# Mixture routes: two doubling ladders replaced by scans, tile sums laid out expert by expert

## The reference, cut to what matters

```python
raw_weights = softmax(flat_x @ gate_w + gate_b)          # mixture 0
top_w, top_idx = top_k(raw_weights, 2)
...
_, topk_idx = top_k(probs, 2)                            # mixture 1
for i in range(N_EXPERTS):
    mask = (topk_idx == i).any(-1)
    sel = sort(where(mask, tok, T))[:capacity]
    ...
    out = out.at[sel].set(yi, mode='drop')
```

## Time and profile before

| what | value |
|---|---|
| median of 3 runs | 2750.04 us (2747.57 to 2751.27) |
| the profiled execution | 2749.84 us |
| its span in the profile | 2748.1 us |
| busy share of PE, DVE, ACT, POOL | 90%, 73%, 57%, 47% |
| mean granted clock of TensorE | 0.946 of full speed |

### The profile page before, as it was taken

The page is one execution under the profiler, slowest core; times in us unless marked ns, Lnnn a source line. Parts: engine busy times, 40 slices in busy tenths (PEclk is TensorE's granted clock), DMA queues, the critical chain, the costliest instruction groups (busy, mean ns, idle before and its releaser), DMA issues. The chain is left out here.

```text
span 2748.1 us, 54258 instructions
## 1 busy us (share of the span) xinstructions
PE 2467.7 (90%) x20834; PEld 1914.0 (70%) x20834; DVE 2001.7 (73%) x2977; ACT 1572.5 (57%) x2642; POOL 1294.0 (47%) x738
## 2 busy tenths in 40 slices
PE   4879939999978999857999999999999999956998
PEld 3658839999977878744666666666666666546998
DVE  5775567888868866537777777777777777277886
ACT  4554426777755543323666666666666666634775
POOL 0000002222224301334888888888888888802443
PEclk9999969999999999986999999999999999957999
DMA  9985325666656754335000000040000000055775
GB/s 394 367 337 182 121 78 202 239 228 231 232 172 217 235 192 128 112 99 127 17 11 15 17 9 17 9 91 11 15 17 9 17 11 13 2 149 190 239 236 139
DMA packets 112303, 352.23 MB, mean 128 GB/s; under 512 B 21424, under 2 KB 53424, under 8 KB 94704
## 3 DMA queue, kind: packets, MB, share of 16 engines
q1 hardware_dynamic: 88432, 289.79, 30.8%
q0 software_dynamic: 22096, 55.07, 7.7%
q10 hardware_dynamic: 1584, 4.75, 0.4%
HBM read 308.40 MB, written 41.16 MB: 127 GB/s over the span
## 5 line engine op out<-in xcount | busy, mean ns | idle before, releaser
L1233 POOL TENSOR_TENSOR at_pool_sum<-at_pool_sum,at_probs 128x1024 f32<-128x1024 f32 x364 | 866.1, 2379 | 97.1 <-ACT at_probs L1359 55.5
L1388 DVE TENSOR_REDUCE at_part_max<-ps_x 128x2 f32<-128x1024 f32 x624 | 734.5, 1221 | 227.7 <-PE ps_x L1289 227.7
L1359 ACT ACTIVATE at_probs<-ps_s 128x512 f32<-128x512 f32 x1352 | 698.2, 604 | 323.8 <-PE ps_s L1248 295.6
L1248 PE MATMUL ps_s<-at_qst,at_kst 97*128 97x256 f32 x2704 | 517.9, 311 | 5.4 <-ACT at_probs L1359 4.3
L1248 PEld LDWEIGHTS ps_s<-at_qst,at_kst 97*128 97x128 f32 x2704 | 369.3, 190 | 218.1 <-ACT at_probs L1359 125.7
L1265 PE MATMUL ps_oz<-at_probs,k_xhat 128*32 128x256 f32 (+1 forms) x5408 | 391.4, 386 | 0.0
L477 PE MATMUL ps_acc<-adj_hi,y_hi 128*128 128x512 f32 (+1 forms) x728 | 289.8, 398 | 93.0 <-DVE adj_lo L543 62.2
L543 DVE TENSOR_TENSOR adj_lo<-adj_raw,adj_hi 128x1024 fp32r<-128x1024 f32 (+1 forms) x182 | 217.7, 1198 | 165.1 <-ACT adj_hi L319 162.8
L479 PE MATMUL ps_acc<-adj_hi,y_lo 128*128 128x512 f32 (+1 forms) x728 | 278.1, 382 | 0.0
L478 PE MATMUL ps_acc<-adj_lo,y_hi 128*128 128x512 f32 (+1 forms) x728 | 278.0, 382 | 0.0
L937 ACT ACTIVATE ex_hid<-ps_ex_h,ex_b 128x256 f32<-128x256 f32 x424 | 193.4, 475 | 124.3 <-PE ps_ex_h L878 113.2
(11 more groups left out here) (223 smaller groups left out, 3998.7 us busy)
## 6 DMA issues: line engine op xcount, KB each, us to landing
ex_w<-w SPq DMA_DIRECT2D x106, 1024.0 KB, 7.7
adj_raw<-adjT SPq DMA_DIRECT2D x156, 512.0 KB, 4.4
k_xhat<-adj SPq DMA_DIRECT2D x26, 1664.0 KB, 7.7
at_qst<-qk_parts SPq DMA_DIRECT2D x78, 128.0 KB, 2.7
results<-ex_res POOLq DMA_DIRECT2D x33, 256.0 KB, 3.3
ex_b<-b SPq DMA_DIRECT2D x53, 128.0 KB, 2.3
adj_raw<-adjT_tail SPq DMA_DIRECT2D x26, 256.0 KB, 2.7
qk_parts<-qk_hi POOLq DMA_DIRECT2D x26, 256.0 KB, 2.8
```

The source lines that it names most:

```text
L1233: pool.tensor_tensor(pool_sum[:, g % 2], pool_sum[:, g % 2], probs[:, tile % RING], ALU.add).then_inc(pool_added, 1)
L1248: last = pe.matmul(ps_s[:, unit % S_BANKS, hh, :], kst[:, 2 * j + hh, k * P:(k + 1) * P], qst[:, g % 2, 2 * j + hh, :], start=True, stop=True)
L1359: act.activation(probs[:, tile % RING, 2 * j:2 * j + 2], ps_s[:, unit % S_BANKS], ACT.Exp, scale=scale).then_inc(taken, 1)
L1388: dve.tensor_reduce(part_max[:, g % 2, heads, qt, kc], ps_x[:, pair, :], AX.X, ALU.max).then_inc(x_free, 1)
```

## The change

- `before` holds other numbers: GpSimd fills it with zeros (one more memset, `MADE` is 14) and writes -1 where the other token of the tile is the token itself or stands behind it. The product with `mask` is then minus the number of tokens of the tile that chose the expert at or behind this token.
- TensorE reads `mask` expert by expert (`p t e -> p e t`, so that neighbours lie 8 numbers, 32 bytes, apart), and both products lie in PSUM expert by expert.
- In `ranks`, the copy of the tile sums, the memset, and the five rounds are replaced by one `tensor_tensor_scan` over 208 numbers: state = `same` * state + tile sum, where `same` is 1 but for the first tile of every expert, where it is 0. It gives the sums up to and with the own tile. The addition of the rank within the tile reads both operands with a step of 26 numbers.
- The running sum over the experts is one scan over 8 numbers in place of the copy, the memset and three rounds.
- `same` and the leading zero of `ends` are set by three memsets on VectorE, ahead of its wait for the exponential.

```diff
@@ make_constants
+    c.inc(pool.memset(m.before[:], 0.0))
     c.settle(pool)
...
-    c.inc(pool.affine_select(out=m.before[:], in_=m.ones[:], compare_op=ALU.is_gt, fill=0.0, base=0,
+    c.inc(pool.affine_select(out=m.before[:], in_=m.before[:], compare_op=ALU.is_gt, fill=-1.0, base=0,
                              pattern=[[1, P]], channel_multiplier=-1))
@@ mixture_routes
             do(dve.tensor_tensor(key[:], mask[:], over_experts(best[:]), ALU.subtract))
+            c.inc(dve.memset(ends[:, 0:1], 0.0))
+            c.inc(dve.memset(same[:], 1.0))
+            c.settle(dve)
+            c.inc(dve.memset(same[:, :, 0:1], 0.0))
             dve.wait_ge(c_act, 1)
...
-                c.inc(dve.memset(carry[:, :, 0, :], 0.0))
-                do(dve.tensor_copy(carry[:, 0, 1:, :], ps[:, 1, 0:W].rearrange("p (t e) -> p t e", e=EXPERTS)))
-                at, step = 0, 1
-                while step < NT:
-                    c.inc(dve.tensor_copy(carry[:, 1 - at, 1:1 + step, :], carry[:, at, 1:1 + step, :]))
-                    do(dve.tensor_tensor(carry[:, 1 - at, 1 + step:, :], carry[:, at, 1 + step:, :], carry[:, at, 1:NT + 1 - step, :], ALU.add))
-                    at, step = 1 - at, 2 * step
-                do(dve.tensor_tensor(rank[:], carry[:, at, 0:NT, :],
-                                     ps[:, 0, 0:W].rearrange("p (t e) -> p t e", e=EXPERTS), ALU.add))
-                return carry[:, at, NT, :]
+                do(dve.tensor_tensor_scan(so_far[:].rearrange("p e t -> p (e t)"), same[:].rearrange("p e t -> p (e t)"), ps[:, 1, 0:W], 0.0,
+                                          ALU.mult, ALU.add))
+                do(dve.tensor_tensor(rank[:], so_far[:].rearrange("p e t -> p t e"), ps[:, 0, 0:W].rearrange("p (e t) -> p t e", t=NT), ALU.add))
+                return so_far[:, :, NT - 1]
...
-            c.inc(dve.memset(ends[:, :, 0:1], 0.0))
-            do(dve.tensor_copy(ends[:, 0, 1:], full[:]))
-            at, step = 0, 1
-            while step < EXPERTS:
-                c.inc(dve.tensor_copy(ends[:, 1 - at, 1:1 + step], ends[:, at, 1:1 + step]))
-                do(dve.tensor_tensor(ends[:, 1 - at, 1 + step:], ends[:, at, 1 + step:], ends[:, at, 1:EXPERTS + 1 - step], ALU.add))
-                at, step = 1 - at, 2 * step
+            do(dve.tensor_tensor_scan(ends[:, 1:], m.ones[:, 0:EXPERTS], full[:], 0.0, ALU.mult, ALU.add))
...
-                flat = mask[:].rearrange("p t e -> p (t e)")
-                pe.matmul(ps[:, 0, 0:W], m.before[:], flat, start=True, stop=True)
-                pe.matmul(ps[:, 1, 0:W], m.ones[:], flat, start=True, stop=True).then_inc(c_pe, 1)
+                marks = mask[:].rearrange("p t e -> p e t")
+                pe.matmul(ps[:, 0, 0:W].rearrange("p (e t) -> p e t", t=NT), m.before[:], marks, start=True, stop=True)
+                pe.matmul(ps[:, 1, 0:W].rearrange("p (e t) -> p e t", t=NT), m.ones[:], marks, start=True, stop=True).then_inc(c_pe, 1)
```

More of the change, by code:

```diff
@@ L64, in settle @@
         eng.wait_ge(self.sem, self.value)
-MADE = 13
+MADE = 14
 def make_constants(pool, m, iota_i, made):
@@ L643, in mixture_routes @@
         rank, best, total = sb("rank", [P, NT, EXPERTS]), sb("best", [P, NT]), sb("total", [P, NT])
-        carry = sb("carry", [P, 2, NT + 1, EXPERTS])
+        so_far, same = sb("so_far", [P, EXPERTS, NT]), sb("same", [P, EXPERTS, NT])
         steps, full = sb("steps", [P, EXPERTS, NCH]), sb("full", [P, EXPERTS])
-        ends, base = sb("ends", [P, 2, EXPERTS + 1]), sb("base", [P, EXPERTS])
+        ends, base = sb("ends", [P, EXPERTS + 1]), sb("base", [P, EXPERTS])
         fine = sb("fine", [P, NT])
@@ L728, in _ @@
             do(dve.tensor_reduce(full[:], steps[:], AX.X, ALU.add))
-            c.inc(dve.memset(ends[:, :, 0:1], 0.0))
-            do(dve.tensor_copy(ends[:, 0, 1:], full[:]))
-            at, step = 0, 1
-            while step < EXPERTS:
-                c.inc(dve.tensor_copy(ends[:, 1 - at, 1:1 + step], ends[:, at, 1:1 + step]))
-                do(dve.tensor_tensor(ends[:, 1 - at, 1 + step:], ends[:, at, 1 + step:], ends[:, at, 1:EXPERTS + 1 - step], ALU.add))
-                at, step = 1 - at, 2 * step
-            do(dve.tensor_tensor(owner[:], ends[:, at, 1:].rearrange("p (a e) -> p a e", a=1).broadcast_to([P, chunks, EXPERTS]),
+            do(dve.tensor_tensor_scan(ends[:, 1:], m.ones[:, 0:EXPERTS], full[:], 0.0, ALU.mult, ALU.add))
+            do(dve.tensor_tensor(owner[:], ends[:, 1:].rearrange("p (a e) -> p a e", a=1).broadcast_to([P, chunks, EXPERTS]),
                                  m.iota[:, 0:chunks].rearrange("p (n a) -> p n a", a=1).broadcast_to([P, chunks, EXPERTS]), ALU.is_le))
@@ L739, in _ @@
             do(dve.tensor_scalar(m.owner[:, 0:chunks], owner_f[:], float(EXPERTS - 1), None, ALU.min))
-            do(dve.tensor_scalar(base[:], ends[:, at, 0:EXPERTS], float(CHUNK), None, ALU.mult))
+            do(dve.tensor_scalar(base[:], ends[:, 0:EXPERTS], float(CHUNK), None, ALU.mult))
             do(dve.tensor_tensor(rank[:], rank[:], by_expert(base[:]), ALU.add))
```

## The result

The changed kernel takes 2742.39 us (median of 7 runs, 2741.37 to 2743.90), against 2750.04 (7 runs, 2747.24 to 2751.27): ratio 0.9975, 95% interval 0.9964 to 0.9985. That is 7.65 us less, by the interval 4 to 10; 2742.3 us was predicted. Timed again later it was 2749.07 against 2756.96, ratio 0.997 (0.9959 to 0.998).

What follows compares the result with a forecast made beforehand. VectorE's instruction list was taken to bound two route blocks, 48.2 us or 1.8% of the span. Savings of 6.15 us (tiles) and 1.6 us (experts) made 7.75 us, giving 2742.3 us; 8-in-10 range 2739.5 to 2747.5.

Steps and rivals of the forecast that it cites:

- What sets the blocks' ends, and that all behind them moves along: Ends of both route blocks: VectorE arrives last, gap 0.90 us, so shortening its list brings every later block forward.
- The ladder over the tiles: Copy and five rounds in each `ranks` call: 2.68 us replaced by a 0.60 us scan plus gap, saving 6.15 us in all.
- The ladder over the experts: Running sum over experts, two calls: 1.01 us replaced by 0.21, saving 0.80 us each, 1.6 us in all.
- The rank addition: VectorE addition in `ranks`, operands read 104 bytes apart: no extra cost taken; upper bound 0.22 us a call, 0.65 in all.
- The rule that I had weighed only for a rival: SBUF reads: full bandwidth needs two hits to a 16-byte line; cited under the strided-read rival, chance 0.16.
- The products on TensorE: Two matmuls per `ranks` call reading `mask` with a 32-byte step: no extra cost taken; upper bound 1.72 us a call.
- The rival's doubling of the records: Strided `mask` read doubles all four TensorE records: 5.2 us go back, 2747.4 us, no measurable change; chance 0.16.
- The memsets: VectorE memsets before the exponential: about 0.41 us a block, hidden by a 0.53 us wait, so no cost.
- TensorE's clock behind the block: Expert products after each route block: start and clock rise come earlier together; a moved lag costs or wins 0.4 us a block.
- The sum: Whole kernel: 6.15 + 1.6 = 7.75 us saved, giving 2742.3 us, 0.28% less.
- A scan at the reciprocal's pace: Rival for the scan over the tiles: 1.54 us each, 4.9 us saved in all, 2745.1 us; chance 0.07.
- GpSimd handing back semaphores: Rival: it ends the first route block, so mixture 0's 2.85 us is not won; 4.9 us saved, 2745.1 us; chance 0.05.

## Why the prediction was right, step by step

- **What sets the blocks' ends, and that all behind them moves along.** Right. The gaps at the ends stayed 0.89 us, and eleven scans for one lengthened the first block by exactly their time. In the second block 0.42 us more came, unexplained. That all behind moves along is shown to a few us by the two kernels with 24 more products, no finer.
- **The ladder over the tiles.** Right: 2.68 us went, and one scan is 0.586 us where I took 0.60. By the Trainium skill (DVE: opcode table, instruction layouts, handler registers and perf-mode slots, section 6) the built-in scan runs at half throughput. The trace agrees: from 8 numbers (0.176 us) to 208 (0.586) the scan takes 2.05 ns a number, and the instructions of the earlier trace rows from 7 (0.157) to 208 (0.375) take 1.08.
- **The ladder over the experts.** Right: 0.80 us a block, and 0.81 and 0.78 when it was put back.
- **The rank addition.** Mis-sized: I took nothing and it costs 0.19 us a call, 0.57 in all, just below my upper bound of 0.22. The reason I gave, that broadcast operands run at full pace, was no evidence: their neighbours lie 0 or 4 bytes apart, and the runs show steps of up to 8 bytes free and those from 16 on not. The rule that I had weighed only for a rival was the right one here.
- **The products on TensorE.** The size was nearly right (0.07 us a call against nothing), and the reason in the main, that the slow clock leaves room: at 1.2 GHz the step costs 8%, at 2.4 GHz it more than doubles a record. The room was smaller than I took it for. My 2.07 ns a column came from a first record that takes longer than those behind it; in a row they need 1.67 ns a column at 1.2 GHz (0.347 us), just under the 1.8 of a stepped read. The rival's doubling of the records is real at 2.4 GHz, but its price of 5.2 us doubles slow records; at the full clock it would be some 0.8 us a call, 2.4 in all.
- **The memsets.** Hidden, as said, and the waits behind them ended 0.07 us earlier, which I had not foreseen.
- **TensorE's clock behind the block.** The lag from the first expert product to the shorter ones went from 4.2 and 3.4 us to 3.8 and 3.2 (415.44 to 419.23, 2494.90 to 2498.05), less than the 0.8 us allowed. From profile to profile it can move further: the clock rose 31.2 to 33.9 us behind the start of the experts of mixture 0.
- **The sum.** 7.14 us in the blocks against 7.75: 0.57 for the additions and 0.21 for TensorE less, 0.14 for the waits more, and 0.03 since a ladder over the tiles gave 2.06 us and not 2.05. The median moved by 7.65; that it fits the forecast to 0.1 us is luck, since the other stages scatter by whole microseconds.
- **The rivals.** A scan at the reciprocal's pace, 1.54 us, was excluded by the first profile (0.586). GpSimd handing back semaphores isn't the bound down to a block of 18.03 us, where the gap is still 0.89.

## What to carry to other kernels

Where a block between two barriers follows one engine's list, its gain can be summed from rows to some tenths of a microsecond, and its length is a far sharper measure than the time of the program. A layout that saves instructions still pays for every stepped operand in SBUF: count each read and write, on each engine, and ask at which clock TensorE will be when it reads. A doubling ladder of small copies and additions is a good place for a scan, since each small instruction of this list cost 0.15 to 0.2 us however few its numbers: here two scans of 0.59 and 0.18 us stood in for ladders of 2.68 and 1.01.

## What the runs showed of the hardware

- VectorE, 208 fp32 numbers, SBUF operand read or written: 0.37 us with neighbours 4 or 8 bytes apart, 0.52 at 16 and 32, 0.55 at 104. The same step of 104 bytes in PSUM: 0.37.
- VectorE writing 208 bf16 numbers 52 bytes apart: 1.08 us, against 0.38 side by side, so 3.4 ns more a number, where an fp32 write loses 0.7 at 16 and 32 bytes and 0.9 at 104.
- TensorE reading its moving operand with steps of 32 bytes (fp32) or 16 (bf16): 1.8 and 1.7 ns a number, at either clock for fp32.
- VectorE's wait for ScalarE's signal ended 0.02 to 0.03 us after the exponential with three memsets ahead of it, and 0.10 us after it without them.
- TensorE's granted clock in attention rose either 51.4 to 51.7 or 54.8 to 55.2 us after the stage's start, with stage lengths of 1179.0 to 1179.6 and 1180.6 to 1181.5 us, in kernels that don't differ there.
